# MLP of a transformer block: the quantisation unit of the GELU's normalised tile and its inverse, on GpSimd as a power, in place of VectorE

## The chip, the cores and the metric

The kernel runs as one program on one core of a Trainium2 chip. The core has five engines that run their own instruction streams and meet at semaphores: TensorE (matmuls; PE in the rows, PEld for its weight loads), VectorE (DVE), ScalarE (ACT), GpSimd (POOL) and SyncE (SP, which here issues DMAs). The metric is the time of one execution on the device, in microseconds. Lower is better. A profile is one execution in which each instruction's start and duration were recorded.

## The reference

Two layers work on x, 4 x 1024 tokens of 256 channels: a cross-attention with an FFN of experts, then a second cross-attention with an MLP. The change is in the last part:

```python
def act_quant_fake(x):
    scale = 127.0 / jnp.clip(jnp.max(jnp.abs(x), axis=-1, keepdims=True), 1e-05)
    return jnp.clip(jnp.round(x * scale), -128.0, 127.0) / scale

def bitlinear(x, w, b):
    dqx = act_quant_fake(x)
    dqw = weight_quant_fake(w)
    return jnp.einsum('btd,hd->bth', dqx, dqw) + b

h = layernorm(x, ln1_g, ln1_b)
h = bitlinear(h, w1, b1)                 # 256 -> 1024
h = jax.nn.gelu(h, approximate=False)
h = layernorm(h, ln2_g, ln2_b)           # over 1024
h = bitlinear(h, w2, b2)                 # 1024 -> 256
```

For each token the second `act_quant_fake` needs the largest absolute value m of 1024 numbers. Its unit is max(m, 1e-5)/127; the numbers are multiplied by the inverse of the unit and rounded, and the product with w2 is multiplied by the unit at the end.

## The kernel before, in words

The tokens are 32 tiles of 128, one token on each partition. The last phase, `mlp_phase`, takes them through all engines as a pipeline. Every engine has a function `step(t, u, has)`, and `run` calls it for t = -6 to 31; in step t each engine works on several tiles, given as t + n, and u or 1 - u picks one of two buffers. What an engine does within a step is in the order of the code; only semaphores connect the engines. The order in step t is:

- **ScalarE**: `squares(t+3)` (sum of squares of the GELU), `h_turned(t+1)` (copy of the transposed tile out of PSUM), `gelu(t+4)`, every second step `x_turned`, in the other early steps `norm_x`, and last `h_rounded(t+2)`, which multiplies the normalised tile `hn` by the inverse unit and rounds it (L1991). It waits for `hs_ok`, which `inverse_h` counts up.
- **VectorE**: `result(t)` (product times unit plus x, from PSUM, L2064); `units(t)`, the same quantisation for x rows of later tiles: in turn `largest_x` twice (L185), `unit_x` (L190), `inverse_x` (L195), up to tile 31; `scale(t+2)` (L2044); `largest_h(t+2)`, the reduction of 1024 numbers (L2049); `unit_h(t+2)` (L2053); `inverse_h(t+2)`, a reciprocal (L2058); `centre(t+3)` (L2037). `centre` and `scale` normalise the GELU in two passes of 128x1024 numbers, each with two tensors of SBUF as inputs.
- **GpSimd**: `mean(t+3)` (L1887); a wait for `affine`, which is the end of `scale(t+2)` on VectorE; `root(t+3)`, which waits for the squares and is a `tensor_scalar` (L1891) and a power to -0.5 (L1893); `rounded(t+7)` of x rows (L200); `turned_scale(t+6)`, a diagonal matrix (L204, `diagonal`); until t = 14 one of `scale_x` (L175) and `shift_x` (L181); once the DMA issue of `offset_x` (L171).
- **TensorE**: `turn_h(t+1)`, 8 transposes of the rounded tile (L1953); `up(t+4)` (L1945); every second step `turn_x` (L1930); `offset(t+5)` (L1938); `down(t+1)`, 8 matmuls (L1960).
- **SyncE**: stores each finished tile of x.

`scale(k)` on VectorE waits for the root of tile k. `centre(k)` waits for its mean. `turn_h(k)` waits for `h_rounded(k)`, and `result(k)` for `down(k)`.

Of the kernel before, what the change touches and what calls it, by code (L numbers as in the profile page):

```python
# [17 lines left out]
ALU = mybir.AluOpType  # L18
# [3 lines left out]
P = 128  # L22
# [56 lines left out]
def count(eng, sem, n):  # L79

    if n > 0:
        eng.wait_ge(sem, n)
# [59 lines left out]
def open_norm(pool, sb, tiles, v, step, to):  # L142
    pool.tensor_scalar(v, sb["mv"][:, tiles, 1], EPS, None, ALU.add).then_inc(step, 1)
    pool.tensor_scalar(sb[to[1]][:, tiles], sb["mv"][:, tiles, 0], -1.0, None, ALU.mult).then_inc(step, 1)


def close_norm(pool, sb, tiles, v, powers, n, step, to):

    rs, nm = sb[to[0]][:, tiles], sb[to[1]][:, tiles]
    pool.wait_ge(step, 4 * n + 2)  # L150
    pool.tensor_tensor(rs, v, powers, ALU.pow).then_inc(step, 1)
    pool.wait_ge(step, 4 * n + 3)
    pool.tensor_tensor(nm, nm, rs, ALU.mult).then_inc(step, 1)
# [13 lines left out]
def offset_x(pool, sb, part):  # L167

    first, behind = OFFSETS[part:part + 2]
    own = sb["b2"][:].rearrange("p (a d) -> p a d", a=1).broadcast_to([P, behind - first, D])  # L170
    pool.dma_start(sb["x"][:, first:behind, :], own, accum_op=ALU.add).then_inc(sb["biased"][part], 16)  # L171


def scale_x(pool, sb, t, step):
    pool.tensor_tensor(sb["ha"][:, t, :], sb["ha"][:, t, :], sb["g1"][:], ALU.mult).then_inc(step, 1)  # L175


def shift_x(pool, sb, t, n, step):

    pool.wait_ge(step, n)  # L180
    pool.tensor_tensor(sb["ha"][:, t, :], sb["ha"][:, t, :], sb["c1"][:], ALU.add).then_inc(step, 1)  # L181
# [16 lines left out]
def round_x(pool, sb, t, done):  # L198
    tile = sb["ha"][:, t, :]
    pool.tensor_scalar(tile, tile, sb["sa"][:, 2, t:t + 1], MAGIC, ALU.mult, ALU.add).then_inc(done, 1)  # L200


def diagonal(pool, sb, t, done):
    pool.tensor_scalar(sb["dg"][t % 2][:], sb["ident"][:], sb["sa"][:, 2, t:t + 1], 1.0, ALU.mult,  # L204
                       ALU.mult).then_inc(done, 1)
# [1615 lines left out]
def mlp_phase(nc, dram, sb):  # L1821
# [5 lines left out]
    with ExitStack() as ctx:  # L1827
        sem = lambda n: ctx.enter_context(nc.semaphore(n + "_m"))
        sbt = lambda n, s, d=F32: ctx.enter_context(nc.sbuf_tensor(n + "_m", s, d))
# [8 lines left out]
        ha, sa, dg = sb["ha"], sb["sa"], sb["dg"]  # L1838
        last = slice(T - ST, T)
        vr, powers = sbt("var", [P, ST]), sbt("powers", [P, ST])  # L1840
        own = range(XT, T)
        qat = [sb["qat_first"], sbt("qat_second", [P, 2, G, P], BF16)]
        ge = [sbt(f"ge{i}", [P, HID]) for i in range(2)]
# [3 lines left out]
        sc = [sbt(f"sc{i}", [P, 8]) for i in range(2)]  # L1847
# [9 lines left out]
        col = lambda s, n: s[:, n:n + 1]  # L1857
        def run(step):
            for t in range(-LEAD, T):
                step(t, t % 2, lambda k: 0 <= t + k < T)  # L1860

        @block.sync
        def _(sp):
            for t in range(T):
                sp.wait_ge(y_ok, t + 1)
                sp.dma_start(out[t * P:(t + 1) * P, :], tile(t)).then_inc(stored, 16)
            sp.wait_ge(stored, 16 * T)

        @block.gpsimd
        def _(pool):  # L1870
            pool.memset(powers[:], -0.5).then_inc(half_ok, 1)
            pool.wait_ge(half_ok, 1)
            open_norm(pool, sb, last, vr[:], factor_step, ("rs_x", "nm_x"))
            close_norm(pool, sb, last, vr[:], powers[:], 0, factor_step, ("rs_x", "nm_x"))

            def rounded(t):
                pool.wait_ge(x_inverse, t // QUAD)
                round_x(pool, sb, t, qx_ok)

            def turned_scale(t):  # L1880
                pool.wait_ge(x_inverse, t // QUAD)
                pool.wait_ge(up_ps, t - 1)
                diagonal(pool, sb, t, diag_ok)

            def mean(t, u):
                pool.wait_ge(gelu_ok, t + 1)
                pool.tensor_scalar(col(se[u], 1), col(se[u], 0), -1.0 / HID, None, ALU.mult).then_inc(mean_ok, 1)  # L1887

            def root(t, u):
                pool.wait_ge(squared, t + 1)  # L1890
                pool.tensor_scalar(col(se[u], 3), col(se[u], 2), 1.0 / HID ** 3, EPS, ALU.mult, ALU.add).then_inc(var_ok, 1)  # L1891
                pool.wait_ge(var_ok, t + 1)
                pool.tensor_tensor(col(se[u], 4), col(se[u], 3), powers[:, 0:1], ALU.pow).then_inc(rooted, 1)  # L1893

            def step(t, u, has):
                if has(3):
                    mean(t + 3, 1 - u)
                if has(2):
                    pool.wait_ge(affine, t + 3)
                if has(3):  # L1900
                    root(t + 3, 1 - u)
                if has(7) and t + 7 >= QUAD:
                    rounded(t + 7)
                if has(6) and t + 6 >= READY:
                    turned_scale(t + 6)
                n = (t + 5) // 2
                if 0 <= n < len(own):
                    if (t + 5) % 2 == 0:
                        pool.wait_ge(x_normed, n + 1)
                        scale_x(pool, sb, XT + n, x_step)  # L1910
                    else:
                        shift_x(pool, sb, XT + n, t + 5, x_step)
                if t == len(own) + 3:
                    pool.wait_ge(x_normed, len(own))
                    offset_x(pool, sb, len(OFFSETS) - 2)

            run(step)

        @block.tensor
# [111 lines left out]
        @block.vector  # L2031
        def _(dve):
            def centre(t, u):

                dve.wait_ge(mean_ok, t + 1)
                count(dve, qct_ps, t - 1)
                dve.scalar_tensor_tensor(hn[u][:], ge[u][:], col(se[u], 1), sb["g2"][:],  # L2037
                                         ALU.add, ALU.mult).then_inc(centred, 1)

            def scale(t, u):  # L2040

                dve.wait_ge(rooted, t + 1)
                dve.wait_ge(centred, t + 1)
                dve.scalar_tensor_tensor(hn[u][:], hn[u][:], col(se[u], 4), sb["c2"][:],  # L2044
                                         ALU.mult, ALU.add).then_inc(affine, 1)

            def largest_h(t, u):
                dve.wait_ge(affine, t + 1)
                dve.tensor_reduce(col(sc[u], 0), hn[u][:], AX.X, ALU.max, apply_absolute_value=True).then_inc(hmax_ok, 1)  # L2049

            def unit_h(t, u):
                dve.wait_ge(hmax_ok, t + 1)
                dve.tensor_scalar(col(sc[u], 1), col(sc[u], 0), sb["clip"][:, 1:2], 1.0 / 127.0, ALU.max,  # L2053
                                  ALU.mult).then_inc(hs1_ok, 1)

            def inverse_h(t, u):
                dve.wait_ge(hs1_ok, t + 1)
                dve.reciprocal(col(sc[u], 2), col(sc[u], 1)).then_inc(hs_ok, 1)  # L2058

            def result(t, u):  # L2060
                dve.wait_ge(down_ps, t + 1)
                if t in OFFSETS:
                    dve.wait_ge(sb["biased"][OFFSETS.index(t)], 16)
                dve.scalar_tensor_tensor(tile(t), pY[:, 0:D], col(sc[u], 1), tile(t), ALU.mult, ALU.add).then_inc(y_ok, 1)  # L2064

            def units(t):

                q, phase = (t + 10) // QUAD, (t + 10) % QUAD
                if not 1 <= q < T // QUAD:
                    return  # L2070
                if phase < 2:
                    first = q * QUAD + 2 * phase
                    count(dve, x_step, 2 * (first + 2 - XT))
                    largest_x(dve, sb, first, 2, x_max)
                elif phase == 2:
                    dve.wait_ge(x_max, 2 * q)
                    unit_x(dve, sb, slice(q * QUAD, (q + 1) * QUAD), x_unit)
                else:
                    dve.wait_ge(x_unit, q)
                    inverse_x(dve, sb, slice(q * QUAD, (q + 1) * QUAD), x_inverse)  # L2080

            def step(t, u, has):
                if has(0):
                    result(t, u)
                units(t)
                if has(2):
                    scale(t + 2, u)
                    largest_h(t + 2, u)
                    unit_h(t + 2, u)
                    inverse_h(t + 2, u)  # L2090
                if has(3):
                    centre(t + 3, 1 - u)

            run(step)


# [128 lines left out]
```

## Time and profile before

| | us |
|---|---|
| three executions, timed | 917.55, 919.96, 921.17 |
| their median | 919.96 |
| profiled execution, first to last instruction | 918.7 |
| busy over the span: TensorE, VectorE | 813.9, 731.9 |
| busy over the span: ScalarE, GpSimd | 600.9, 592.8 |

The profiled execution is known by its span alone; the timed ones include a little around it. Busy time is what the engine's instructions last; waiting for a semaphore is not in it. An instruction that has started but waits for access to memory is counted as busy, so a long duration is not always work.

### The profile page before, as it was taken

The numbers are of one execution on the slowest core, as the hardware profiler recorded it, in microseconds if no ns is written. First come the engines' busy times: TensorE is split into PE (matmuls) and PEld (weight loads), VectorE is DVE, ScalarE is ACT, GpSimd is POOL, SyncE is SP. The second block draws the span as 40 slices with busy tenths as digits, with TensorE's granted clock in tenths as the row PEclk, the third lists the DMA queues.
The fourth block names the chain that finished last, engine by engine and source line by source line (L and its number), as shares of the span: only waits on it lengthen the run. The fifth ranks groups of instructions, "written<-read, shape, count | busy, mean of one in ns | idle before, by whom it ended". The sixth has DMA issues, their size and how long they took to land. (4 is left out here: it accounts for less than half of the span.)

```text
span 918.7 us, 24387 instructions
## 1 busy us (share of the span) xinstructions
PE 813.9 (89%) x9252; PEld 661.7 (72%) x9252; DVE 731.9 (80%) x1597; ACT 600.9 (65%) x1106; POOL 592.8 (65%) x731
## 2 busy tenths in 40 slices
PE   5699999899788888699998599999998879999996
PEld 4587878788667677699998587778787645555564
DVE  3688988788666666578885788889889859999996
ACT  2366777666544443277873166777676679999995
POOL 2344777755335545347777588689989878777551
PEclk9799999999999999899999889999999999999996
DMA  8464599700011212356762856300301120004000
GB/s 267 73 260 168 217 391 384 308 2 2 2 37 72 88 62 86 98 169 205 223 204 101 286 124 92 48 3 2 48 2 21 29 36 24 24 30 81 29 29 29
DMA packets 55634, 100.04 MB, mean 109 GB/s; under 512 B 10208, under 2 KB 36448, under 8 KB 55520
## 3 DMA queue, kind: packets, MB, share of 16 engines
q1 hardware_dynamic: 38672, 70.12, 22.7%
q0 software_dynamic: 15232, 27.80, 11.9%
q8 instruction: 75, 1.23, 0.6%
q10 hardware_dynamic: 1616, 0.58, 0.3%
q14 instruction: 39, 0.32, 0.1%
HBM read 35.04 MB, written 59.24 MB: 103 GB/s over the span
## 5 line engine op out<-in xcount | busy, mean ns | idle before, releaser
L578 POOL TENSOR_TENSOR sm_a<-sm_a,mx_a 128x616 f32<-128x616 f32 x128 | 158.1, 1235 | 101.6 <-DVE mx_a L972 100.2
L874 ACT ACTIVATE pr_a<-sm_a 128x616 f32<-128x616 f32 x128 | 91.6, 715 | 87.0 <-POOL sm_a L578 87.0
L1259 POOL DMA_INDIRECT slots<-sx,idx_f x64 | 65.0, 1015 | 70.6 <-DVE idx_f L1652 53.5
L1265 POOL DMA_INDIRECT mixed<-rep,qidx_f x80 | 78.0, 975 | 47.4 <-DVE rep L1759 24.2
L747 PE MATMUL pT_a<-ident,pr_a 128*128 128x128 f32 x640 | 97.6, 283 | 9.4 <-ACT pr_a L874 5.0
L972 DVE TENSOR_REDUCE mx_a<-sm_a 128x8 f32<-128x616 f32 x128 | 99.0, 773 | 0.0
L770 PE MATMUL pO_a<-aw,ot_a 128*128 128x256 f32 x256 | 73.1, 409 | 20.4 <-DVE ot_a L993 19.7
L747 PEld LDWEIGHTS pT_a<-ident,pr_a 128*128 128x128 f32 x640 | 72.0, 143 | 24.4 <-issue 17.0
L721 PE MATMUL pA_a<-sx,aw 128*128 128x128 f32 x512 | 72.6, 288 | 0.5 <-ACT sx L868 0.5
L770 PEld LDWEIGHTS pO_a<-aw,ot_a 128*128 128x128 f32 x256 | 43.9, 191 | 39.3 <-DVE ot_a L993 35.9
L721 PEld LDWEIGHTS pA_a<-sx,aw 128*128 128x128 f32 x512 | 66.5, 203 | 1.5 <-ACT sx L868 1.2
L1938 PE MATMUL pS<-b,dg 128*128 128x512 f32 x124 | 58.6, 595 | 3.3 <-POOL dg L204 1.7
L965 DVE TENSOR_TENSOR sm_a<-pS_a,mask 128x616 f32<-128x616 f32 x64 | 50.4, 791 | 13.0 <-PE pS_a L732 13.0
L883 ACT ACTIVATE V<-pT_a 128x512 f32<-128x512 f32 (+1 forms) x96 | 46.7, 518 | 19.6 <-PE pT_a L747 19.5
L965 DVE TENSOR_TENSOR sm_a<-pS,mask 128x616 f32<-128x616 f32 x64 | 50.3, 790 | 8.8 <-PE pS L732 8.7
L883 ACT ACTIVATE rep<-pT_a 128x512 f32<-128x512 f32 (+1 forms) x96 | 46.6, 518 | 14.0 <-PE pT_a L747 13.9
L762 PE MATMUL pO_a<-rep,V 128*32 128x128 f32 x1024 | 52.5, 277 | 1.0 <-DVE x L998 1.0
L762 PE MATMUL pO_a<-V 128*32 128x128 f32 x1024 | 52.4, 277 | 1.0 <-DVE x L998 1.0
L762 PE MATMUL pO_a<-rep,sel 128*32 128x128 f32 x1024 | 51.6, 274 | 0.0
L762 PE MATMUL pO_a<-V,sel 128*32 128x128 f32 x1024 | 51.6, 274 | 0.0
L584 POOL TENSOR_TENSOR x<-x,bo 128x256 f32<-128x256 f32 x64 | 48.1, 752 | 0.0
L1953 PE MATMUL pC_m<-ident,hn_m 128*128 128x128 f32 x256 | 36.7, 289 | 8.9 <-ACT hn_m L1991 8.2
(348 smaller groups left out, 2517.0 us busy)
## 6 DMA issues: line engine op xcount, KB each, us to landing
slots<-sx SPq DMA_DIRECT2D x16, 2176.0 KB, 9.4
sx<-slots SPq DMA_DIRECT2D x40, 272.0 KB, 3.2
x<-x_in SPq DMA_DIRECT2D x4, 1024.0 KB, 11.2
x<-mixed POOLq DMA_DIRECT2D x4, 1024.0 KB, 10.1
out_x<-x SPq DMA_DIRECT2D x32, 128.0 KB, 1.7
rep<-gu_in SPq DMA_DIRECT2D x10, 256.0 KB, 4.6
aw<-aw_in SPq DMA_DIRECT2D x2, 1024.0 KB, 7.3
ha<-mixed SPq DMA_DIRECT2D x2, 1024.0 KB, 7.2
```

Source lines behind the costliest of these rows:

```text
L578: pool.tensor_tensor(heads, heads, mx[u][:, g, :].rearrange("p (h a) -> p h a", a=1).broadcast_to([P, HG, SK]), ALU.subtract).then_inc(shi ...
L721: mm = pe.matmul(pA[:, D + g * P:D + (g + 1) * P], aw[:, k, g * P:(g + 1) * P], xt[u][:, k * P:(k + 1) * P], start=(k == 0), stop=(k == G ...
L747: mm = pe.transpose(pT[:, (J * t + j) % 2, (n % 4) * P:(n % 4 + 1) * P], pr[u][:, g, c * P:(c + 1) * P], sb["ident"][:])
L762: mm = pe.matmul(pO[own, at:at + P], left, pt[u][:, g * CK + c, :], start=(g == 0 and r == 0 and what == 0), stop=(r == 1), skip_group_che ...
L770: mm = pe.matmul(pO[:, 0:D], ot[u][:, k * P:(k + 1) * P], aw[:, k, 3 * D:4 * D], start=(k == 0), stop=(k == G - 1), skip_group_check=True)
L874: act.activation(pr[u][:, g, 0:NS], sm[u][:, g, :], ACT.Exp).then_inc(exped, 1)
L883: act.activation(pt[u][:, lo:lo + n, :].rearrange("p n t -> p (n t)"), pT[:, (J * t + j) % 2, 0:n * P], ACT.Copy).then_inc(pt_sb, 1)
L965: dve.tensor_tensor(sm[u][:, g, :].rearrange("p (b h k) -> p b h k", b=ROWS_OF_HEADS, k=SK), pS[:, :, g * QS:(g + 1) * QS].rearrange("p b ...
L972: dve.tensor_reduce(mx[u][:, g, :], sm[u][:, g, :].rearrange("p (h k) -> p h k", k=SK), AX.X, ALU.max).then_inc(maxed, 1)
L1259: pool.indirect_dma_start(dram["slots"][:], bass.IndirectOffsetOnAxis(idx[:, at:at + 1], 0), rows[g % 2][:, j, :], None).then_inc(moved[g ...
L1265: pool.indirect_dma_start(dram["mixed"][:], bass.IndirectOffsetOnAxis(qidx[:, at:at + 1], 0), ys[q % 2][:, j, :], None).then_inc(out_moved ...
L1938: pe.matmul(pU[u][:, half_row], dg[u][:], sb["b1"][:, half_row], start=True, stop=False)
```

## The change

`unit_h` and `inverse_h` leave VectorE's step and stand in GpSimd's, directly after `root(t+3)` and ahead of `rounded(t+7)`. `unit_h` keeps its form. `inverse_h` becomes a `tensor_tensor` power with a column of -1.0 (`minus`), since GpSimd had done its root in this way already. The column is filled once at the start of the phase. The semaphores are the same: `hmax_ok` (reduction done), `hs1_ok` (unit done), `hs_ok` (inverse done).

```diff
+        minus = sbt("minus", [P, 1])
...
             pool.memset(powers[:], -0.5).then_inc(half_ok, 1)
-            pool.wait_ge(half_ok, 1)
+            pool.memset(minus[:], -1.0).then_inc(half_ok, 1)
+            pool.wait_ge(half_ok, 2)
...
+            def unit_h(t, u):
+                pool.wait_ge(hmax_ok, t + 1)
+                pool.tensor_scalar(col(sc[u], 1), col(sc[u], 0), sb["clip"][:, 1:2], 1.0 / 127.0, ALU.max,
+                                   ALU.mult).then_inc(hs1_ok, 1)
+
+            def inverse_h(t, u):
+                pool.wait_ge(hs1_ok, t + 1)
+                pool.tensor_tensor(col(sc[u], 2), col(sc[u], 1), minus[:], ALU.pow).then_inc(hs_ok, 1)
...
                 if has(3):
                     root(t + 3, 1 - u)
+                if has(2):
+                    unit_h(t + 2, u)
+                    inverse_h(t + 2, u)
                 if has(7) and t + 7 >= QUAD:
                     rounded(t + 7)
...
-            def unit_h(t, u):
-                dve.wait_ge(hmax_ok, t + 1)
-                dve.tensor_scalar(col(sc[u], 1), col(sc[u], 0), sb["clip"][:, 1:2], 1.0 / 127.0, ALU.max,
-                                  ALU.mult).then_inc(hs1_ok, 1)
-
-            def inverse_h(t, u):
-                dve.wait_ge(hs1_ok, t + 1)
-                dve.reciprocal(col(sc[u], 2), col(sc[u], 1)).then_inc(hs_ok, 1)
...
                     scale(t + 2, u)
                     largest_h(t + 2, u)
-                    unit_h(t + 2, u)
-                    inverse_h(t + 2, u)
```

GpSimd in two steps of the middle, before. `se` holds mean, variance and root of a tile, `sc` its maximum, unit and inverse:

```order
L1887 TENSOR_SCALAR se0_m<-se0_m 128x1
L1891 TENSOR_SCALAR se0_m<-se0_m 128x1
L1893 TENSOR_TENSOR se0_m<-se0_m,powers_m 128x1
L200 TENSOR_SCALAR ha<-ha,sa 128x256
L204 TENSOR_SCALAR dg1<-ident,sa 128x128
L175 TENSOR_TENSOR ha<-ha,g1 128x256
L1887 TENSOR_SCALAR se1_m<-se1_m 128x1
L1891 TENSOR_SCALAR se1_m<-se1_m 128x1
```

And the same place now:

```order
L1889 TENSOR_SCALAR se0_m<-se0_m 128x1
L1893 TENSOR_SCALAR se0_m<-se0_m 128x1
L1895 TENSOR_TENSOR se0_m<-se0_m,powers_m 128x1
L1899 TENSOR_SCALAR sc1_m<-sc1_m,clip 128x1
L1904 TENSOR_TENSOR sc1_m<-sc1_m,minus_m 128x1
L200 TENSOR_SCALAR ha<-ha,sa 128x256
L204 TENSOR_SCALAR dg1<-ident,sa 128x128
L175 TENSOR_TENSOR ha<-ha,g1 128x256
```

Unit and inverse of the tile in buffer 1 stand between the root of the next tile, in buffer 0, and the rounding of x rows.

VectorE at the same place, before; `hn` is the normalised tile, `sa` the x rows' counterpart of `sc`:

```order
L2049 TENSOR_REDUCE sc0_m<-hn0_m 128x1
L2053 TENSOR_SCALAR sc0_m<-sc0_m,clip 128x1
L2058 RECIPROCAL sc0_m<-sc0_m 128x1
L2037 SCALAR_TENSOR_TENSOR hn1_m<-ge1_m,se1_m,g2 128x1024
L2064 SCALAR_TENSOR_TENSOR x<-pY_m,sc1_m,x 128x256
L185 TENSOR_REDUCE sa<-ha 128x2
L2044 SCALAR_TENSOR_TENSOR hn1_m<-hn1_m,se1_m,c2 128x1024
L2049 TENSOR_REDUCE sc1_m<-hn1_m 128x1
```

And now:

```order
L2063 TENSOR_REDUCE sc0_m<-hn0_m 128x1
L2051 SCALAR_TENSOR_TENSOR hn1_m<-ge1_m,se1_m,g2 128x1024
L2069 SCALAR_TENSOR_TENSOR x<-pY_m,sc1_m,x 128x256
L185 TENSOR_REDUCE sa<-ha 128x2
L2058 SCALAR_TENSOR_TENSOR hn1_m<-hn1_m,se1_m,c2 128x1024
L2063 TENSOR_REDUCE sc1_m<-hn1_m 128x1
```

The reduction is now followed at once by `centre` of the next tile.

## Rows read from the trace of the kernel before

**Rows 1.** The page's first line.

```profile
span 918.7 us, 24387 instructions
```

**Rows 2.** Stretches of the MLP: length, busy us (instructions) by engine, granted clock.

```profile
754.59:775.06 20.47, 19.23 (x98) 11.32 (x99) 18.82 (x27) 18.72 (x29) 19.40 (x28) 1.00 0.06 20
775.06:835.67 60.61, 56.72 (x313) 35.42 (x312) 58.18 (x84) 57.98 (x85) 46.33 (x74) 1.00 0.08 27
835.67:875.17 39.50, 37.22 (x208) 23.36 (x207) 37.83 (x55) 36.34 (x52) 22.74 (x42) 1.00 0.31 61
875.17:903.43 28.26, 25.48 (x145) 15.83 (x143) 26.59 (x37) 26.84 (x39) 13.53 (x25) 1.00 0.09 29
903.43:918.70 15.27, 9.34 (x40) 6.42 (x40) 6.95 (x11) 4.91 (x5) 0.76 (x2) 0.51 0.08 27
```

**Rows 3.** The chain of waits, 875 to 885 us: start, us, what.

```profile
875.17 1.23 DVE sc_m L2049
...
876.87 1.16 ACT hn_m L1991
...
878.08 1.09 PE pC_m L1953 x8
...
880.03 0.44 PE pA_m L1930 x4
880.47 1.72 PE pS L1938 x4
882.19 0.89 PE pY_m L1960 x8
...
883.50 1.29 DVE hn_m L2044
...
884.81 1.23 DVE sc_m L2049
```

**Rows 4.** Timeline of VectorE and GpSimd, 795 to 800 us: start, us, instruction.

```profile
795.31 1.22 DVE L2049 TENSOR_REDUCE sc_m<-hn_m 128x1 f32<-128x1024 f32 x1
795.37 0.19 POOL L1891 TENSOR_SCALAR se_m<-se_m 128x1 f32<-128x1 f32 x1 [1.96 <-DVE hn_m L2044]
...
795.64 0.58 POOL L1893 TENSOR_TENSOR se_m<-se_m,powers_m 128x1 f32<-128x1 f32 x1
...
796.32 0.48 POOL L200 TENSOR_SCALAR ha<-ha,sa 128x256 f32<-128x256 f32 x1
...
796.78 0.38 POOL L204 TENSOR_SCALAR dg<-ident,sa 128x128 f32<-128x128 f32 x1
...
796.90 1.32 DVE L2037 SCALAR_TENSOR_TENSOR hn_m<-ge_m,se_m,g 128x1024 f32<-128x1024 f32 x1
...
797.12 1.69 POOL L181 TENSOR_TENSOR ha<-ha,c 128x256 f32<-128x256 f32 x1
...
798.54 0.67 DVE L185 TENSOR_REDUCE sa<-ha 128x2 f32<-128x512 f32 x1
...
799.13 1.27 DVE L2044 SCALAR_TENSOR_TENSOR hn_m<-hn_m,se_m,c 128x1024 f32<-128x1024 f32 x1
```

**Rows 5.** The line of `mean` on GpSimd: duration in ns, least/median/most.

```profile
L1887 POOL TENSOR_SCALAR se_m<-se_m x32: 217/1146/1267, 751.2 to 900.7; 128x1 f32<-128x1 f32 x32
```

**Rows 6.** The same timeline at the first tiles.

```profile
756.43 1.45 POOL L1893 TENSOR_TENSOR se_m<-se_m,powers_m 128x1 f32<-128x1 f32 x1
...
757.96 1.28 DVE L2044 SCALAR_TENSOR_TENSOR hn_m<-hn_m,se_m,c 128x1024 f32<-128x1024 f32 x1
757.98 1.60 POOL L200 TENSOR_SCALAR ha<-ha,sa 128x256 f32<-128x256 f32 x1
...
759.91 0.73 POOL L181 TENSOR_TENSOR ha<-ha,c 128x256 f32<-128x256 f32 x1
```

**Rows 7.** The line of the power on four columns: duration in ns, least/median/most.

```profile
L151 POOL TENSOR_TENSOR rs_x<-var_m,powers_m x1: 1045/1045/1045, 748.2 to 748.2; 128x4 f32<-128x4 f32 x1
```

**Rows 8.** Timeline of ScalarE at the last tiles.

```profile
905.13 1.15 ACT L1991 ACTIVATE hn_m<-hn_m,sc_m 128x1024 f32<-128x1024 f32 x1 [1.14 <-DVE sc_m L2058]
```

## Prediction

> **What bounds the kernel now.** I read the page's first rows, then the stretches of the MLP, the chain of waits through two of its tiles, and the timelines of VectorE and GpSimd. The page gives 918.7 us from the first to the last instruction [rows 1]; the runs' median, 919.96, lies 1.3 us above, so the sum is made on the span and 1.3 is added. The change touches only the MLP, from about 747 us on.
>
> The stretches are cut at starts of `largest_h`: I write L(k) for its start on tile k and H(k) for the start of `h_rounded` on ScalarE. L(0) is 754.59, L(4) 775.06, L(16) 835.67, L(24) 875.17, L(30) 903.43 [rows 2]. The middle needs 60.61/12 = 5.05 us a tile. There VectorE is busy for 58.18 (96%) and ScalarE for 57.98, that is 4.83 a tile. Both look full, which invites the reading that any microsecond taken from VectorE is won. The chain says more. From L(24) to L(26) it runs: reduction, `unit_h`, `inverse_h`, H(24) at 876.87, turning of the tile 878.08, up product, turning of x 880.03, offset 880.47, down product 882.19, done at 883.1, `result`, `scale` on VectorE at 883.50, L(26) at 884.81 [rows 3]. So `h_rounded` of a tile leads, through one whole step of TensorE and `result`, to the `scale` of the tile two further on. The path has no real gap and takes 884.81 - 875.17 = 9.64 us for two tiles, 4.82 a tile. Its piece from L to H is 876.87 - 875.17 = 1.70.
>
> With the work on x rows that VectorE does between `result` and `scale` the path explains the middle too. It is 0.59 long where `largest_x` stands (798.54 to 799.13, [rows 4]). For even tiles `largest_x` and `unit_x` alternate; `unit_x` adds about 0.2. Four tiles are 2 x 9.64 + 0.59 + 0.2 = 20.07, and a third of 60.61 is 20.20. The path from L to H to the second next L sets the pace, VectorE and ScalarE a little under it. For odd tiles no turning of x is in TensorE's step (880.47 - 880.03 = 0.44), 9.20 instead of 9.64.
>
> **The change, part by part.** *Removed from VectorE*: `unit_h` and `inverse_h`, 32 each. Two operations with no wait between them overlap by 0.08 on VectorE (a reduction of 0.67 at 798.54, the next start at 799.13, [rows 4]), so `centre` of the next tile starts 1.22 - 0.08 = 1.14 after L, where it starts now at 796.90 - 795.31 = 1.59. That saves 0.45 a tile, on VectorE alone. None of it is on the path above.
>
> *Added to GpSimd*: a `tensor_scalar` and a power on 128x1. The first is 0.19, as the variance of the same shape (795.37, [rows 4]), the second 0.57 by the root, which is a power of the same shape (795.64, 0.58, [rows 4]). The power to -1 itself is not in the trace. From below the nearest row is a `tensor_scalar` of this shape, 0.19 [rows 4]; from above a power on four columns, 1.04 [rows 7]. I take 0.57, since shape, engine and operation are the root's. A dependent step costs 0.08 more.
>
> *When it can run* is the main term. `unit_h` waits for the reduction's end and reaches GpSimd about 0.09 after it, at L + 1.31: GpSimd's wait for `scale` ended at 795.37, 0.06 after VectorE's own next start at 795.31, which is some 0.03 after the end [rows 4]. `centre` has started at L + 1.14, and `centre` and `scale` each read two tensors of SBUF. What GpSimd starts behind such an operation stands still until it is over: `rounded` started at 757.98, 0.02 after `scale` (757.96, 1.28), and took 1.60 [rows 6], against 0.48 free (796.32, [rows 4]); `mean`, one column, has a least of 217 ns and a median of 1146 ns [rows 5]; `shift_x` at 797.12, 0.22 behind `centre`, took 1.69 [rows 4]. What GpSimd starts first goes through: `diagonal` at 796.78, 0.12 ahead of `centre`, took 0.38, and `centre` 1.32 [rows 4]. Small operations end about 0.09 after the blocking one. So `unit_h` ends at L + 1.14 + 1.27 + 0.09 = 2.50, `inverse_h` runs from 2.58 to 3.15, and H = L + 3.20, where it was L + 1.70. **The path gets 1.50 longer.**
>
> The Trainium skill, "SBUF — State Buffer", section "Who interferes with whom", says the same of the order: a VectorE instruction with two SBUF inputs contends with a GpSimd instruction that reads SBUF, and issue order, not shape, decides who blocks. The trace agrees (0.02 behind: 1.60 us; 0.12 ahead: 0.38). Had the wait been shorter than the reduction's own overlap, `unit_h` would win and H would be L + 2.20.
>
> *The steady stretches.* Two tiles are now 9.64 + 1.50 = 11.14 for even tiles, 10.70 for odd ones. VectorE (5.05 - 0.45) and ScalarE (4.83) are both under 5.57, so the even path decides. L(24) is 875.17 and L(16) 835.67 [rows 2]: 39.50 becomes 4 x 11.14 + 0.85 for x rows = 45.4, **+5.9**.
>
> In the middle GpSimd also has `scale_x` or `shift_x`. After `inverse_h` (L + 3.15) come `rounded` 0.48, `diagonal` 0.38 and that operation, 0.73 where free (759.91, [rows 6]): it runs from about L + 4.05 to 4.78, while the next `scale` is due between L + 4.1 and 4.6. Carrying tiles 4 to 9 on by hand with these durations, `scale` waits for it by 0.04 to 0.47 and once `diagonal` falls behind `scale`; L(4) to L(8) comes to 23.6, that is 5.9 a tile. Three such fours are 70.8 instead of 60.6, **+10.2**. The DMA issue of `offset_x` near tile 15 keeps GpSimd for over a microsecond once more: **+0.8**.
>
> *The first tiles.* Here GpSimd is late already. The root of tile 1 starts at 756.43 behind `centre` and takes 1.45 [rows 6]; `unit_h` of tile 0 then stands where `rounded` stood, just behind `scale` (757.96). It ends at 759.33 and `inverse_h` at 759.98, so H(0) is 760.0, some 3.7 late. Carried on: H(1) 765.7, L(2) 765.0, L(3) 773.4, L(4) 779.2 against 775.06, **+4.1**.
>
> *The last tiles.* L(24) to L(28) is 22.3 instead of 19.3, +3.0; the last two, where TensorE has less in its step, +0.3. H(30) was L(30) + 1.70 (903.43, 905.13, [rows 2, 8]). The squares of tile 31 now come late, its root falls behind `centre`, and `unit_h` of tile 30 queues behind that root: H(30) about L(30) + 4.1, +2.4. After it the end is a string of single waits, as long as now, 13.6. **+5.7** together.
>
> One more memset of one column before the first norm: 0.1, counted as nothing. The wait added before `unit_h` holds on GpSimd `rounded` and `diagonal`, for which TensorE has over 2 us in hand; and `result` needs only the unit, earlier than the inverse.
>
> Sum: 5.9 + 10.2 + 0.8 + 4.1 + 5.7 = 26.7. Span 918.7 + 26.7 = 945.4; with 1.3 around it **946.7**.
>
> **The rivals.** *A: `unit_h` slips in ahead of `centre`.* Then H = L + 2.20, the path +0.50, for 15 turns of two tiles +7.5, with the ends about +8.5: **928.5**. For it: the margin is 0.17 us. Against: 0.02 was enough [rows 6], and both starts follow from the same reduction.
>
> *B, not slower: VectorE is the bound, and the path has slack.* Then 0.45 a tile is won until ScalarE's 4.83 holds: 60.61 to 57.98, 39.50 to 36.34, 28.26 to 26.84 [rows 2], together -7.2: **912.8**. Its place is the wait of `h_rounded`; it decides if the inverse is back by L + 1.70 or ScalarE can take it later at no cost. Against it: even an unblocked unit and power need 0.09 + 0.19 + 0.08 + 0.57 behind the reduction, 0.45 more than now, and the path is full at 9.64. The Trainium skill, "Perfetto Trace Analysis", section "Optimizing Scalar/DVE Operations", holds that offloading from a saturated VectorE may help, and warns that between VectorE and GpSimd it might not, as they share a port. By its first half it would be B; the rows speak for the warning.
>
> *C: GpSimd stays behind for good.* With `unit_h` behind `scale` in each tile, as in the first, H - L stays near 4 and more in the middle: 12 tiles at 6.5 instead of 5.9, +7, and a power of 1.04 gives 0.47 x 15.5 = +7.3 whatever else: **954 to 961**. A power of 0.19 gives -5.9: **940.8**.
>
> *D: no gain, no loss*, the waits being hidden after all: 920.
>
> **How the numbers follow.** My case 0.78, with its own range 938 to 955 (the two prices of the power, and half the price of the middle); C 0.09; A 0.07; B 0.04; D 0.02. The range 928 to 960 leaves out B and D, part of C and a possible fall of TensorE's clock: it is granted 1.00 in all stretches but the last [rows 2], where the engine mostly waits, and its share falls in the middle from 0.94 to about 0.8. Half a per cent is about what a measurement of this kernel can tell from no change. Faster by more than that 0.04, within it 0.03, slower 0.93.
>
> **What would show it.** In the changed profile: `unit_h` near 1.2 us in the mean, not 0.19; `inverse_h` near 0.57; `centre` 1.14 after the start of the reduction; H - L near 3.2; ScalarE idle before `h_rounded` for 0.7 us or more in nearly each tile, released by GpSimd; two tiles 11.1 apart near the end and four 23 to 24 apart in the middle; VectorE idle before `result`, released by TensorE. I am wrong if `unit_h` takes 0.2, if H can come 1.5 later without moving the second next L, or if the power to -1 costs something else.

## The result and the profile after

| | before | changed |
|---|---|---|
| timed, us | 917.55 to 921.17, median 920.56 (4) | 945.78 to 952.12, median 950.62 (4) |
| profiled execution, first to last instruction | 918.7 | 950.3 |
| L(0) to the end, us | 164.1 | 194.4 |

The ratio is 1.0329, with a 95% interval of 1.0295 to 1.0363: 3.3% slower. A second set of runs, with another profile, gave 1.0314 (1.0282 to 1.0345). Forecast were 946.7 us, in a range of 928 to 960.

In the changed kernel `unit_h` is L1899, `inverse_h` L1904, `mean` L1889, `root` L1893 and L1895; `centre` is L2051, `scale` L2058, `largest_h` L2063, `result` L2069; `h_rounded` is L2005; TensorE has `turn_h` L1967, `up` L1959, `turn_x` L1944, `offset` L1952, `down` L1974. The stretches cut at L(0), L(4), L(16), L(24) and L(30), as in [rows 2] (length, busy us and instructions of PE, PEld, DVE, ACT, POOL, granted clock of TensorE, DMA):

```profile
755.87:782.70 26.83, 20.66 (x93) 12.59 (x96) 18.05 (x19) 18.03 (x28) 21.55 (x36) 0.87 0.04 15
782.70:852.53 69.83, 56.93 (x308) 35.43 (x312) 54.34 (x60) 58.72 (x85) 60.16 (x98) 1.00 0.07 24
852.53:901.55 49.02, 41.16 (x207) 25.96 (x210) 35.09 (x39) 37.51 (x53) 32.79 (x59) 0.93 0.25 49
901.55:933.43 31.88, 24.54 (x134) 14.91 (x135) 24.64 (x25) 25.17 (x36) 22.07 (x37) 1.00 0.08 26
933.43:950.30 16.87, 9.60 (x48) 6.94 (x48) 6.37 (x7) 6.75 (x8) 3.36 (x7) 0.66 0.07 24
```

The middle went from 60.61 to 69.83 us with VectorE 3.84 us less busy: what was taken from the busiest engine came back as waiting, and more. The two tiles of [rows 3] in the changed kernel, by the chain of waits (start, us, what):

```profile
901.55 1.23 DVE sc_m L2063
...
902.88 1.27 POOL sc_m L1899
...
904.23 0.56 POOL sc_m L1904
...
904.82 1.16 ACT hn_m L2005
...
906.02 1.09 PE pC_m L1967 x8
...
908.41 1.72 PE pS L1952 x4
910.13 0.89 PE pY_m L1974 x8
...
911.44 1.29 DVE hn_m L2058
...
912.75 1.23 DVE sc_m L2063
```

From one L to the second next are 912.75 - 901.55 = 11.20 us (9.64 before), and H - L is 904.82 - 901.55 = 3.27 (1.70 before). The timeline of VectorE, GpSimd and ScalarE at the same place shows why (start, us, instruction, idle time ahead of it and who ended it):

```profile
901.55 1.22 DVE L2063 TENSOR_REDUCE sc_m<-hn_m 128x1 f32<-128x1024 f32 x1
...
902.69 1.27 DVE L2051 SCALAR_TENSOR_TENSOR hn_m<-ge_m,se_m,g 128x1024 f32<-128x1024 f32 x1
902.88 1.27 POOL L1899 TENSOR_SCALAR sc_m<-sc_m,clip 128x1 f32<-128x1 f32 x1 [0.44 <-DVE sc_m L2063]
...
904.23 0.56 POOL L1904 TENSOR_TENSOR sc_m<-sc_m,minus_m 128x1 f32<-128x1 f32 x1
...
904.82 1.15 ACT L2005 ACTIVATE hn_m<-hn_m,sc_m 128x1024 f32<-128x1024 f32 x1 [1.98 <-POOL sc_m L1904]
```

`centre` starts 1.14 after the reduction, `unit_h` 0.19 behind `centre`. It works on one column and takes 1.27, as long as `centre`. Odd tiles are different: there `unit_h` mostly comes behind the root's power and takes 0.30 to 1.0, so its mean is 0.86. Two tiles are paced by the even one; the odd one has time in hand.

### The profile page after: what moved, and what is told of

The parts are those of the page before. It is cut to its first block and busy times, and to the rows that moved or that the text cites. A ratio compares the mean times of both kernels' runs of the same rounds, so it can differ in the third digit from the quotient of the medians.

```text
span 950.3 us, 24373 instructions
## 1 busy us (share of the span) xinstructions
PE 819.5 (86%) x9237; PEld 665.6 (70%) x9252; DVE 722.6 (76%) x1533; ACT 603.2 (63%) x1106; POOL 630.4 (66%) x796
## 5 line engine op out<-in xcount | busy, mean ns | idle before, releaser
L1967 PE MATMUL pC_m<-ident,hn_m 128*128 128x128 f32 x256 | 37.8, 295 | 33.9 <-ACT hn_m L2005 33.8
L1952 PE MATMUL pS<-b,dg 128*128 128x512 f32 x124 | 59.2, 600 | 2.7 <-POOL dg L204 1.8
L1967 PEld LDWEIGHTS pC_m<-ident,hn_m 128*128 128x128 f32 x256 | 30.1, 150 | 43.4 <-ACT hn_m L2005 43.3
L883 ACT ACTIVATE V<-pT_a 128x512 f32<-128x512 f32 (+1 forms) x96 | 46.7, 518 | 20.8 <-PE pT_a L747 20.7
L2005 ACT ACTIVATE hn_m<-hn_m,sc_m 128x1024 f32<-128x1024 f32 x32 | 36.7, 1148 | 32.8 <-POOL sc_m L1904 32.7
L2069 DVE SCALAR_TENSOR_TENSOR x<-pY_m,sc_m,x 128x256 f32<-128x256 f32 x32 | 15.5, 483 | 48.5 <-PE pY_m L1974 48.5
```

Of the source, the lines that this page charges most:

```text
L883: act.activation(pt[u][:, lo:lo + n, :].rearrange("p n t -> p (n t)"), pT[:, (J * t + j) % 2, 0:n * P], ACT.Copy).then_inc(pt_sb, 1)
L1952: pe.matmul(pU[u][:, half_row], dg[u][:], sb["b1"][:, half_row], start=True, stop=False)
L1967: mm = pe.transpose(pC[:, k * P:(k + 1) * P], hn[u][:, k * P:(k + 1) * P], sb["ident"][:])
```

## The experiments

Each kernel is described by its difference from the changed kernel, or, where said, from the kernel before. On the chip of the first four runs all that lies ahead of the MLP took some 33 us longer (the kernel before 954.0 there, L(0) of the variants at 787 to 790), so they are read by their ratio to the kernel before on the same chip and by the stretches of the MLP. No profile of the kernel before was taken on that chip; its stretches are those of the other one. e8 and e9 were executed once each, 932.05 and 946.06 us, so of them only the stretches are read. The last rows are TensorE's granted clock:

| us | before | changed | changed, again | e1 | e2 | e3 | e4 | e5 | e6 | e8 | e9 |
|---|---|---|---|---|---|---|---|---|---|---|---|
| L(0) to L(4) | 20.5 | 26.8 | 27.0 | 22.9 | 24.8 | 24.8 | 25.0 | 19.8 | 20.5 | 22.0 | 24.9 |
| L(4) to L(16) | 60.6 | 69.8 | 70.2 | 69.5 | 69.3 | 72.2 | 69.7 | 59.4 | 62.1 | 61.3 | 69.3 |
| L(16) to L(24) | 39.5 | 49.0 | 49.0 | 46.7 | 46.1 | 45.4 | 45.1 | 38.4 | 41.0 | 45.3 | 49.0 |
| L(24) to L(30) | 28.3 | 31.9 | 31.9 | 31.4 | 30.9 | 32.2 | 30.6 | 27.7 | 28.3 | 30.6 | 31.9 |
| L(30) to the end | 15.3 | 16.9 | 16.9 | 16.3 | 16.4 | 15.6 | 16.7 | 13.7 | 15.0 | 17.5 | 16.9 |
| L(0) to the end | 164.1 | 194.4 | 195.0 | 186.8 | 187.5 | 190.2 | 187.1 | 158.9 | 166.8 | 176.7 | 192.1 |
| H - L, even tiles near the end | 1.70 | 3.27 | 3.27 | 3.11 | 2.95 | 2.31 | 3.98 | 1.9 to 2.8 | 1.71 | 3.99 | 3.26 |
| clock, L(0) to L(4) | 1.00 | 0.87 | 0.87 | 1.00 | 0.93 | 1.00 | 0.86 | 1.00 | 1.00 | 1.00 | 0.93 |
| clock, L(16) to L(24) | 1.00 | 0.93 | 0.93 | 0.96 | 0.96 | 1.00 | 0.96 | 1.00 | 1.00 | 0.92 | 0.93 |

**Is it GpSimd's operations or their standing still? One run takes an operation out of GpSimd, one makes an operation cheap.**

```diff
 # e1, unit back on VectorE
 # GpSimd's step
                 if has(2):
-                    unit_h(t + 2, u)
                     inverse_h(t + 2, u)
 # VectorE's step
                     largest_h(t + 2, u)
+                    unit_h(t + 2, u)
```

> The changed kernel with the unit back on VectorE; only the inverse (the power) stays on GpSimd. L is the start of the reduction of a tile, H that of its rounding on ScalarE. Theory (what is dear is that GpSimd stands still behind VectorE's next large operation): the unit ends at L + 1.47, the next tile's centring starts at L + 1.39, the power reaches GpSimd at about L + 1.56, behind it, and ends 0.43 after it, at L + 3.09: H = L + 3.13 against 3.27 in the changed kernel. Two tiles near the end 11.05 us, the whole about 948 us. The power should last 1.5 us in the mean, not 0.57. Rival (what is dear is the duration of GpSimd's two operations and the hand-overs): H = L + 2.2, two tiles near 10.1 and the whole about 934 us.

Measured: ratio 1.0261 (1.0224 to 1.0298), that is +24.9 us where the changed kernel has about +30; H - L 3.11. The timeline, here 944 to 948 us:

```profile
944.77 1.22 DVE L2057 TENSOR_REDUCE sc_m<-hn_m 128x1 f32<-128x1024 f32 x1
...
946.02 0.21 DVE L2061 TENSOR_SCALAR sc_m<-sc_m,clip 128x1 f32<-128x1 f32 x1
946.15 1.28 DVE L2045 SCALAR_TENSOR_TENSOR hn_m<-ge_m,se_m,g 128x1024 f32<-128x1024 f32 x1
946.37 1.47 POOL L1899 TENSOR_TENSOR sc_m<-sc_m,minus_m 128x1 f32<-128x1 f32 x1
```

The power now starts 0.22 behind `centre` and takes 1.47 (1.06 in the mean, where 1.5 was expected, since in most odd tiles it takes 0.54). With half of what was moved moved back, H - L fell by 0.16 only: the price is one wait for `centre`, and whichever operation comes first pays it. The theory's 3.13 and 11.05 for two tiles came out; the rival's 2.2 did not. The whole fell by 5 us and the stretches by 7.6, where 2 to 3 were expected. This lies in the first tiles (22.9 for 26.8) and in L(16) to L(24) (46.7 for 49.0), the two stretches where TensorE's clock fell less than in the changed kernel. Near the end, at the full clock, two tiles took the 11.05 of the expectation.

```diff
 # e2, the power replaced
-                pool.tensor_tensor(col(sc[u], 2), col(sc[u], 1), minus[:], ALU.pow).then_inc(hs_ok, 1)
+                pool.tensor_scalar(col(sc[u], 2), col(sc[u], 1), 1.0, None, ALU.mult).then_inc(hs_ok, 1)
```

> The changed kernel with the power replaced by a multiplication with 1.0 on GpSimd: the inverse of the unit is not computed, so the output is not the reference's. Prices the power by itself. Theory: 0.57 becomes 0.19, H - L 3.27 becomes 2.89, two tiles near the end 11.20 become 10.82, and with 15.5 turns of two tiles the whole is 6 us shorter, about 944 us. Rival (the power is the dear part, since it is what differs from a reciprocal): most of the 30 us go, under 930 us.

Measured: ratio 1.0253 (1.0210 to 1.0297), +22.6 us where the expectation had about +24 and its rival under +10; H - L 2.95, so 0.32 less, since the multiplication took 0.24 rather than 0.19. The last six tiles gained 0.95 us, three turns of 0.32. In the middle five of the six turns are 0.3 to 0.45 shorter than in the changed kernel; the sixth, L(12) to L(14), is 1.2 longer, and it holds a fall of TensorE's clock. The power is the smaller part of the price, 0.32 of 1.57.

**Taking the hold away by making VectorE wait.**

```diff
 # e3
                 dve.wait_ge(mean_ok, t + 1)
+                count(dve, hs_ok, t)
                 count(dve, qct_ps, t - 1)
```

> The changed kernel with one wait more: VectorE's centring of a tile waits until GpSimd has done the inverse of the tile before. So VectorE stands idle for about 1.1 us in every tile, and nothing it runs is in GpSimd's way. Theory (the hold): the unit lasts 0.2 in every tile, H = L + 2.2. VectorE's own round becomes 5.15 us plus the work on x rows and the path of two tiles 10.1 to 10.2, so the last tiles come every 5.15, the middle every 5.5, and the whole is some 9 us shorter than the changed kernel: about 941 us, although a wait was added. Rival (the hold costs nothing, VectorE's time is what counts): 1.1 us more in each of 31 tiles, about 984 us.

Measured: ratio 1.0314 (1.0282 to 1.0347), +28.4 us. The hold is gone, as its rows near the end show:

```profile
962.79 0.31 POOL L1899 TENSOR_SCALAR sc_m<-sc_m,clip 128x1 f32<-128x1 f32 x1 [0.44 <-DVE sc_m L2064]
...
963.19 0.55 POOL L1904 TENSOR_TENSOR sc_m<-sc_m,minus_m 128x1 f32<-128x1 f32 x1
...
963.77 1.15 ACT L2005 ACTIVATE hn_m<-hn_m,sc_m 128x1024 f32<-128x1024 f32 x1 [1.90 <-POOL sc_m L1904]
...
963.83 1.29 DVE L2052 SCALAR_TENSOR_TENSOR hn_m<-ge_m,se_m,g 128x1024 f32<-128x1024 f32 x1 [1.14 <-POOL sc_m L1904]
```

The unit takes 0.31 and H - L is 2.31. VectorE idles 1.14 us in each tile and the whole is no longer than the changed kernel, so the rival, 31 x 1.1 us more, is out. But the gain of 9 us did not come. The stretches are together 4.3 us shorter than the changed kernel's. But L(0) to L(4) is 2.1 and L(16) to L(24) 3.6 shorter, and there e3 has the full clock and the changed kernel falls of it; in the middle and up to L(30), where both have the full clock, e3 is longer, 72.2 for 69.8 and 32.2 for 31.9. The last six tiles are at 5.36 apiece instead of the 5.15 expected. The middle is at 6.02 instead of 5.5, and there the expectation was wrong. Its rows show what was left out of it:

```profile
844.43 1.28 DVE L2052 SCALAR_TENSOR_TENSOR hn_m<-ge_m,se_m,g 128x1024 f32<-128x1024 f32 x1 [1.15 <-POOL sc_m L1904]
844.45 1.54 POOL L200 TENSOR_SCALAR ha<-ha,sa 128x256 f32<-128x256 f32 x1
...
845.96 0.37 POOL L204 TENSOR_SCALAR dg<-ident,sa 128x128 f32<-128x128 f32 x1
...
846.26 1.85 DVE L2059 SCALAR_TENSOR_TENSOR hn_m<-hn_m,se_m,c 128x1024 f32<-128x1024 f32 x1
846.31 0.72 POOL L175 TENSOR_TENSOR ha<-ha,g 128x256 f32<-128x256 f32 x1
```

The inverse lets `centre` and `rounded` go at the same moment, so `rounded` stands for 1.54, and then two operations of GpSimd pass ahead of `scale`, which takes 1.85 for 1.27. The hold was moved to other operations. So e3 shows where H - L comes from, and not that taking the hold away makes the kernel faster.

**Is the path of two tiles the bound? TensorE's order.**

```diff
 # e4: on the changed kernel. e5: the same on the kernel before
                     if (t + 5) % 2 == 0:
                         turn_x((t + 5) // 2)
-                    offset(t + 5, 1 - u)
                 if has(1) and t > -1:
                     down(t + 1, 1 - u)
+                if has(5) and t > -5:
+                    offset(t + 5, 1 - u)
```

> The changed kernel with one move on TensorE: in each step the product with the offset of a later tile (1.72 us) stands behind the down product instead of ahead of it. The work is the same. Theory (the path rounding of a tile, TensorE's step, result, scale and reduction of the tile two further on sets the pace): it gets 1.72 shorter in two tiles, 11.20 becomes 9.48 near the end, under ScalarE's 4.83 a tile; in the middle GpSimd, which is busy or held for 5.0 of each 5.8 us, becomes the bound at 4.9 to 5.3 a tile. The whole about 931 us. Rival (GpSimd's held operations bound the pace by themselves, the path through TensorE has slack): no change, about 950 us.

Measured: ratio 1.0249 (1.0219 to 1.0280), so +22.6 us for about +30. Near the end a tile takes 5.10 instead of 5.31, in the middle 5.81 instead of 5.82. The timeline near the end names the next bound:

```profile
936.21 1.15 ACT L2006 ACTIVATE hn_m<-hn_m,sc_m 128x1024 f32<-128x1024 f32 x1 [0.16 <-POOL sc_m L1904]
...
938.61 1.30 DVE L2052 SCALAR_TENSOR_TENSOR hn_m<-ge_m,se_m,g 128x1024 f32<-128x1024 f32 x1
938.65 0.19 POOL L1893 TENSOR_SCALAR se_m<-se_m 128x1 f32<-128x1 f32 x1 [0.46 <-ACT sq_m L2011]
...
938.92 1.41 POOL L1895 TENSOR_TENSOR se_m<-se_m,powers_m 128x1 f32<-128x1 f32 x1
...
940.33 0.30 POOL L1899 TENSOR_SCALAR sc_m<-sc_m,clip 128x1 f32<-128x1 f32 x1
```

What holds it is a ring of one tile: rounding, squares, root, unit, inverse, next rounding. It exists because `unit_h` now stands behind the next tile's `root` on GpSimd, and `root` waits for squares that ScalarE makes after the rounding. The root's first operation just passes beside `centre`; its power starts 0.31 behind and stands until `centre` is over, 1.41. This second path was not in the prediction. It lay at 5.1 us, under the 5.6 of the first.

The middle fits the rival's number, and two more runs settle whether GpSimd holds it there. Both leave out the gain and shift of x rows on GpSimd:

```diff
 # e8: on e4. e9: on the changed kernel
-                        scale_x(pool, sb, XT + n, x_step)
+                        pool.sem_inc(x_step, 1)
                     else:
-                        shift_x(pool, sb, XT + n, t + 5, x_step)
+                        pool.sem_inc(x_step, 1)
```

> The changed kernel with the offset product behind the down product, and without the gain and shift of x rows on GpSimd in the MLP (0.73 us in each of 20 steps; left out, so the last ten tiles are not the reference's). In the variant with only the first of these the middle stayed at 5.8 us a tile, and the last tiles took 5.10. Theory: what held the middle there is GpSimd's round, so without these operations it falls to about the 5.10 of the last tiles plus up to 0.35 for x rows on VectorE; L(4) to L(16) 62 to 65 us instead of 69.7. Rival (the path through TensorE is still the bound in the middle): 69 to 70.

> The changed kernel, TensorE's order untouched, without the gain and shift of x rows on GpSimd in the MLP (left out, so the last ten tiles are not the reference's). The counterpart of the same omission with the offset product moved, where the middle fell from 69.7 to 61.3 us. Theory: with TensorE's order untouched the path of two tiles holds the middle, 2 x 11.20 + 0.8 = 23.2 for four tiles, and GpSimd's 0.73 a tile is worth nothing: L(4) to L(16) 69.0 to 69.8. The first four tiles should fall as there, from 26.9 to about 22 to 25. Rival (GpSimd's round holds the middle of the changed kernel): 61 to 65.

Middle of e4, e8 and e9:

```profile
812.26:882.00 69.74, 58.24 (x312) 34.26 (x312) 54.36 (x61) 58.68 (x86) 63.80 (x97) 1.00 0.07 24
```

```profile
775.57:836.89 61.32, 58.22 (x315) 34.25 (x314) 53.70 (x60) 58.66 (x85) 53.26 (x85) 1.00 0.08 27
```

```profile
777.19:846.53 69.34, 57.23 (x309) 35.79 (x314) 53.16 (x60) 59.12 (x86) 50.86 (x85) 1.00 0.07 24
```

With TensorE's order untouched the omission is worth 0.5 us in 12 tiles (e9 against 69.83): the path of two tiles holds the middle. With the path shortened it is worth 8.4 us (e8 against e4): then GpSimd's round holds it, and only with both gone is the middle down to 5.11 a tile. The chain of waits there is for the most part the ring. So the changed kernel has two bounds in the middle at the same height, 5.8 us a tile, and taking away either alone gives nothing. The rival of e4 was right on what e4 would show there; that the path had slack was wrong for the changed kernel.

**The same two questions to the kernel before.** e5 is the move of e4 on the kernel before.

> The kernel before, unit and inverse on VectorE, with the product with the offset behind the down product in TensorE's step. Theory (the path of two tiles is the bound before the change too): it falls from 9.64 to 7.92, and VectorE's own round, 4.52 plus 0.35 for x rows, is next. The middle falls from 5.05 to 4.87 a tile, the stretch of the last tiles from 4.71 to 4.52 plus what ScalarE adds, together 4 to 5 us less than the kernel before, 0.995 of it. Rival (VectorE, busy for 96%, is already the bound): no change.

Measured: ratio 0.9945, 95% interval 0.9920 to 0.9971, median 913.1 us against 919.1. It is faster than both kernels. The middle went from 60.6 to 59.4 us (58.4 expected), 39.5 to 38.4, 28.3 to 27.7. In its middle VectorE is busy for 58.11 of 59.36 us, and its chain of waits from 790 to 812 us holds nothing but VectorE's operations and their issue. One tile of it:

```profile
802.22 1.23 DVE sc_m L2050
...
803.81 1.32 DVE hn_m L2038
...
805.44 0.16 DVE sa L195
805.60 1.21 DVE hn_m L2045
...
806.83 1.23 DVE sc_m L2050
```

So before the change the path and VectorE's own round lay close together: the middle took 5.05 us a tile, and 4.95 with the path shortened and VectorE the bound (4.61 in the tile shown, which has the least work on x rows; others take up to 5.2). The chain of the kernel before has both: from 795 to 802 us it runs on VectorE alone, from there to 815 through ScalarE and TensorE.

```diff
 # e6: on the kernel before
                 if has(0):
                     result(t, u)
-                units(t)
                 if has(2):
                     scale(t + 2, u)
                     largest_h(t + 2, u)
                     unit_h(t + 2, u)
                     inverse_h(t + 2, u)
+                units(t)
```

> The kernel before with VectorE's work on x rows moved from between result and scale to behind the inverse, ahead of the next tile's centring. The work is the same. Theory: it leaves the path of two tiles (which becomes 9.64 without an addition, 4.82 a tile) but stays in VectorE's round (4.87), so the middle falls from 5.05 to 4.87 a tile, 2 to 3 us less in all, near the end nothing; ratio 0.997. Rival (VectorE is the bound): no change at all, since VectorE does the same work.

Measured: ratio 1.0021 (1.0001 to 1.0042), the middle 62.1 us, slower by a little where a small gain was expected. Neither side had it. The rows of one tile:

```profile
806.56 1.85 DVE L2037 SCALAR_TENSOR_TENSOR hn_m<-ge_m,se_m,g 128x1024 f32<-128x1024 f32 x1
806.60 0.73 POOL L181 TENSOR_TENSOR ha<-ha,c 128x256 f32<-128x256 f32 x1
...
807.29 1.20 POOL L1887 TENSOR_SCALAR se_m<-se_m 128x1 f32<-128x1 f32 x1
```

In the middle `centre` is put back by 0.1 to 0.6 us. Once in four tiles `shift_x`, which stood behind `centre` before (1.69, [rows 4]), now keeps up with it and passes free in 0.73, and `centre` takes 1.85 for 1.32; in the other three it takes 1.25 to 1.52. What GpSimd gains VectorE loses: in the middle it is busy for 60.89 us, 2.7 more than before, with the same work. The expectation counted the path and VectorE's round and left out whom `centre` meets.

**The clock, and chance.** The changed kernel was run once more as it is.

> The changed kernel itself, to have it beside the kernel before and the other variants of this call on one chip. The stretch of the MLP from L(0) to the end should be 190 to 194 us against 164 of the kernel before, whatever the time ahead of it is on this chip; H - L 3.27 on even tiles. What I do not know is how often the clock of TensorE falls in it: in its first profile it was granted 0.87 in two stretches of two tiles, each 12.9 to 13.0 us instead of 11.2. If that belongs to the change it comes again, if it is chance it does not.

Measured: 948.4 us, ratio 1.0314, stretches as in the table, each within 0.4 us of the first profile. The step from L(21) to L(22) is 8.38 in the one and 8.39 in the other. TensorE's rows there, in the first profile:

```profile
880.13 1.51 PE L1967 MATMUL pC_m<-ident,hn_m 128*128 128x128 f32 x8 [2.35 <-ACT hn_m L2005]
881.44 1.91 PE L1959 MATMUL pS<-q,qat_second_m 128*128 128x512 bf16 x4
```

After 2.35 us without work the transposes take 1.51 and the up product 1.91; at the full clock, at 906 us, they take 1.09 and 1.03 (durations in the timeline, where one row runs on into the next). The granted clock of 880 to 884 us is 0.58, that is for most of it the lower of the two levels, 1.2 GHz:

```profile
880.00:884.00 4.00, 3.87 (x17) 2.76 (x18) 2.76 (x3) 2.85 (x5) 3.50 (x8) 0.58 0.01 2
```

It lies on the path. Two tiles take 13.01 there, and again 12.88, instead of 11.2. In the second of these the clock is 0.57 from 894 to 898 us, and the chain of waits has

```profile
894.22 1.50 PE pS L1959 x4
895.72 0.85 PE pA_m L1944 x4
896.57 2.35 PE pS L1952 x4
```

where [rows 3] have 0.86, 0.44 and 1.72: 1.7 us more. The first has 1.51, 1.71 and 0.85 for transposes, up product and turning of x, where they have 1.09, 0.86 and 0.44, also 1.7. It belongs to the change: both profiles have it at the same tiles, and e9 too. That the idle time brought the fall was not tried by itself, and its length alone does not settle it: at 906 us TensorE had been idle for 1.89 and no fall came, in e9 for 2.33 at 804.76 and none came, and 3.15 before the first tile's transposes came with a fall in e9 (0.67 over 757 to 762 us) and without one in e8 (1.00 over the same). What brings a fall stays open.

## Why the prediction was right

| term | forecast | first profile | second |
|---|---|---|---|
| first tiles, to L(4) | +4.1 | +6.4 | +6.5 |
| middle, with `offset_x` | +11.0 | +9.2 | +9.6 |
| L(16) to L(24) | +5.9 | +9.5 | +9.5 |
| from L(24) on | +5.7 | +5.2 | +5.2 |
| sum | +26.7 | +30.3 | +30.9 |

What lies ahead of L(0) moved by chance, to 755.9 in the first profile and 751.1 in the second, from 754.6.

- **Path and H - L: right.** 3.27 for 3.20, 11.20 for 11.14. `unit_h` falls behind `centre` by 0.19 for 0.17, on even tiles; its mean, named as a sign with 1.2, is 0.86, since in odd tiles it comes later, behind the root. The power to -1 costs what the root does, 0.56. e1 to e3 show that the larger part of the 1.57 is one wait for `centre`: it goes to 2.31 without it (e3), and to 2.95 with a cheap inverse (e2).
- **That taking 0.45 us from VectorE earns nothing: right.** VectorE is busy for 54.34 of 69.83 us in the middle, where it was 58.18 of 60.61.
- **L(16) to L(24): mis-sized**, +9.5 for +5.9. The last part of the forecast named TensorE's clock as a risk and put it at nothing. Two falls cost 1.7 us each, 3.4 of the 3.6 that are missing.
- **First tiles: mis-sized**, +6.4 for +4.1. H(0) came 5.30 after L(0), as forecast (5.4), but L(2) came 13.8 after L(0) and not 10.4. Most of that is the clock again, granted at 0.51 from 761 to 768 us: in the changed kernel's chain of waits (below) three pieces of TensorE take 5.4, which take 1.09, 0.86 and 0.89, 2.8 in all, in [rows 3]. That is 2.5 of the 3.3. The rest is the path itself: at the full clock H(0) to L(2) needs some 5.9 (8.4 measured, less 2.5), and the working left 5.0; it had passed over that `result` of tile 0, which VectorE does ahead of the `scale` of tile 2, cannot be before the down product of tile 0.

```profile
759.76 1.38 POOL sc_m L1904
...
762.37 1.97 PE pC_m L1967 x8
764.33 1.71 PE pS L1959 x4
766.04 1.71 PE pY_m L1974 x8
```

- **Middle: too dear by 1.8**, 23.3 us for four tiles where 23.6 were worked out, and nothing where 0.8 was put for the DMA issue of `offset_x`. The issue stands at 851.29, at the end of the stretch, and the four tiles that end there take 23.26, as the four before them do (23.25); the four after take 23.1. `scale` was expected to wait for `scale_x` on even tiles too; even tiles kept to their 11.2 plus x rows, and the collisions fell on odd ones, which have time.
- **L(30) on**: H(30) came at L + 4.19, as forecast; the end after it was 0.9 us shorter.
- **The sum** is closer than its terms. Two are too low by 5.9 together, mostly for falls of the clock, and two too high by 2.3; that these cancel in part is luck. The measured time would lie in the range without it too. What the path sets by itself came out: L(16) to L(24) less the falls +6.1 for +5.9, L(24) to L(30) +3.6 for +3.3.
- The rivals: A (`unit_h` slips in) and B (VectorE is the bound) did not occur. C's mechanism occurs in part of the odd tiles, where H - L is 3.8 to 4.9, and never took over. The second bound in the middle, GpSimd's round at 5.8 (e4, e8), was not seen as one; it changed nothing in the time, and in e4 it left the middle at 5.81 although the path was shorter.

## What to carry to other kernels

Before an operation is moved off the busiest engine, follow one result around until it comes back to its own engine: if that path fills the period, a saved microsecond on the busy engine is worth nothing (0.45 a tile here) and an added one is paid in full (1.57 on H - L, 1.56 on two tiles). A small operation on GpSimd that waits for a VectorE operation can meet the next one of VectorE. Here that one reads two tensors of SBUF, and the price was its length, 1.27 for `unit_h` and 1.47 for the power in e1, not the operation's own 0.3 and 0.56. A cheaper repair than moving work between engines was to reorder one: the product that nobody waits for behind the one that the path runs through gave 0.55% (0.29 to 0.80) on the kernel before.

## What the runs showed of the hardware

- Two operations of GpSimd in a row can both pass ahead of VectorE: `scale` at 846.26 took 1.85 in e3, with a diagonal ahead of it and a gain that starts 0.05 behind it and takes its free 0.72; `centre` took 1.85 in e6, again with a diagonal and a shift. The loss is then on VectorE, 0.5 to 0.6 us.
- Within some 0.05 us the start times do not tell who goes first. `rounded` at 844.45, 0.02 behind `centre`, stood for 1.54; the root's first operation at 938.65, 0.04 behind `centre`, took 0.19 and was not held. In the MLP of all the profiles, an operation of GpSimd that started over 0.1 us behind `centre` or `scale`, while these ran, stood until they were over.
- `unit_h` directly behind the root's power (e4, start 940.33, as that ends) takes 0.30; behind `centre` it takes 1.27.
- TensorE's granted clock fell inside stretches that the kernel before passes at 1.00: 0.51 over 761 to 768 us, 0.58 over 880 to 884, 0.57 over 894 to 898, with single idle times of TensorE of 3.87, 2.35 and 2.01 us that end at 762.4, 880.1 and 893.1, and at the same tiles in three profiles (the changed kernel twice, e9). Idle times of 2.33 (e9) and 3.15 (e8) had no fall.
